# A fused graph-attention and transformer kernel: four steps moved at the seam between attention and feed-forward

## What is computed

```python
gamma1, gamma2, scale1, scale2, shift1, shift2 = ada(silu(cond))
x1 = _ln(x) * (scale1 + 1.0) + shift1
q, k, v = x1 @ mat_qkv_w.T + qkv_bias              # 16 heads of 16
q = _l2norm(q) * exp(min(scale_mul, log 100)); k = _l2norm(k)
o = softmax(q @ k.T) @ v
x = x + (o @ proj_w.T + proj_b) * gamma1           # "projection", "gate", "residual"
x2 = _ln(x) * (scale2 + 1.0) + shift2
h = gelu(x2 @ fc1_w.T + fc1_b)                     # 256 -> 1024
x = x + (h @ fc2_w.T + fc2_b) * gamma2             # 1024 -> 256
```

## Time and profile before

| | us |
|---|---|
| time of three runs | 797.12, 798.02, 800.97 (median 798.02) |
| the profiled execution | 799.24 |
| its span in the trace | 797.5 |
| PE busy | 732.4 (92% of the span) |
| DVE / ACT / POOL busy | 500.0 / 444.0 / 323.0 |

### The profile page before, as it was taken

One profiled execution on the slowest core, in us unless ns is written; L12 is line 12 of the kernel. 1 busy time (PEld: TensorE's weight loads), 2 busy tenths in 40 slices (PEclk: granted clock), 3 DMA queues, 4 the chain that ended last, 5 costly groups with the idle time before them and its releaser, 6 DMA issues.

```text
span 797.5 us, 15010 instructions
## 1 busy us (share of the span) xinstructions
PE 732.4 (92%) x4708; PEld 521.8 (65%) x4708; DVE 500.0 (63%) x1047; ACT 444.0 (56%) x733; POOL 323.0 (41%) x550
## 2 busy tenths in 40 slices
PE   4799999999996689999999999998598999999997
PEld 2587778888873345555555555555357888888885
DVE  2158999989987757767676767665414444444432
ACT  0335555555543367766666666666455555555553
POOL 1024655655653245555555555544542202222100
PEclk9989999999999899999999999999779999999999
DMA  8831333333311777667666666677400000000001
GB/s 236 293 93 39 111 100 107 114 97 109 101 32 53 128 156 147 148 147 154 141 153 147 150 147 144 147 145 146 76 14 1 14 27 14 27 28 27 14 27 39
DMA packets 83096, 79.65 MB, mean 100 GB/s; under 512 B 22942, under 2 KB 71710, under 8 KB 83054
## 3 DMA queue, kind: packets, MB, share of 16 engines
q1 hardware_dynamic: 81726, 78.95, 41.2%
q10 hardware_dynamic: 1328, 0.16, 0.1%
HBM read 57.13 MB, written 21.66 MB: 99 GB/s over the span
## 4 chain that ended last, share of the span: by engine, by line
PE 53%; ACT 5%; DVE 3%; DMA 3%; issue 2%; POOL 2%; SPq 1%; ACTq 0%; DVEq 0%; POOLq 0%
PE ps L1667 11%; PE ps L1681 11%; PE ps L1488 7%; PE ps L1560 5%; PE ps L1546 5%; PE ps L1598 3%; ACT probsT L903 3%; PE ps L1498 3%; PE ps L1579 2%; PE ps L1514 1%; DMA k_stack<-parts_dram 1%; PE ps L1652 1%; PE ps L1591 1%; ACT part_pairs L926 1%; DMA gate_rows<-rows_dram 1%
## 5 line engine op out<-in xcount | busy, mean ns | idle before, releaser
L903 ACT ACTIVATE probsT<-ps 128x1024 f32<-128x1024 f32 x128 | 130.5, 1019 | 31.5 <-PE ps L1546 31.5
L1303 DVE TENSOR_TENSOR hidden_low<-hidden,hidden_high 128x512 fp32r<-128x512 f32 x64 | 46.1, 720 | 110.1 <-ACT hidden_high L997 61.6
L994 ACT ACTIVATE hidden<-ps,b_fc 128x512 f32<-128x512 f32 x64 | 44.1, 689 | 74.1 <-PE ps L1667 74.1
L1546 PEld LDWEIGHTS ps<-q_stack,k_stack 49*128 49x128 f32 x512 | 39.4, 190 | 61.6 <-ACT probsT L903 37.1
L1560 PE MATMUL ps<-probsT,v_ones 128*32 128x256 f32 x1024 | 70.5, 395 | 4.7 <-ACT probsT L903 4.5
L1546 PE MATMUL ps<-q_stack,k_stack 49*128 49x256 f32 x512 | 66.1, 337 | 8.7 <-ACT probsT L903 7.6
L691 POOL TENSOR_TENSOR scores<-scores,row_max 128x640 f32<-128x640 f32 x32 | 42.1, 1317 | 77.1 <-DVE row_max L1033 77.1
L1196 DVE TENSOR_REDUCE neg_max<-ps 128x4 bf16<-128x344 f32 x128 | 59.4, 506 | 15.2 <-PE ps L1514 15.2
L1488 PE MATMUL ps<-w_qkv,x1T 128*128 128x512 f32 x128 | 64.7, 628 | 3.2 <-DVE part_pairs L1203 3.2
L1406 PE MATMUL ps<-x_res,w_q 128*128 (+1 forms) x256 | 65.2, 401 | 0.0
L1406 PEld LDWEIGHTS ps<-x_res,w_q 128*128 128x128 f32 x256 | 48.5, 199 | 11.5 <-issue 5.4
(11 more groups left out here) (181 smaller groups left out, 1709.3 us busy)
## 6 DMA issues: line engine op xcount, KB each, us to landing
parts_dram<-part_pairs SPq DMA_DIRECT2D x64, 256.0 KB
q_stack<-parts_dram SPq DMA_DIRECT2D x96, 128.0 KB, 5.4
k_stack<-parts_dram SPq DMA_DIRECT2D x96, 128.0 KB, 5.8
adj<-in_adj SPq DMA_DIRECT2D x16, 440.0 KB, 3.5
xT<-in_xT SPq DMA_DIRECT2D x16, 256.0 KB, 2.8
x_res<-in_x SPq DMA_DIRECT2D x16, 256.0 KB, 3.4
x_in<-in_x SPq DMA_DIRECT2D x16, 256.0 KB, 2.7
gate_rows<-rows_dram SPq DMA_DIRECT2D x16, 256.0 KB, 7.1
```

Source lines behind the costliest of these rows:

```text
L903: nc.scalar.activation(probsT[:, s % 4, :], ps[:, COLS:COLS + 2, :].rearrange("p a n -> p (a n)"), ACT.Exp).then_inc(exp_made, 1)
L994: nc.scalar.activation(hidden[:, s % RAW, :], ps[:, FC1[s % FC1_BANKS], :], ACT.Gelu, bias=b_fc1[:, m:m + 1]).then_inc(gelu_made, 1)
L1303: nc.vector.tensor_tensor(hidden_parts[1][:, s % H_SLOTS, :], hidden[:, s % RAW, :], hidden_parts[0][:, s % H_SLOTS, :], ALU.subtract).the ...
L1546: mm = nc.tensor.matmul(ps[:, COLS + j, kt * N:(kt + 1) * N], k_stack[at, par, s, kt * P:(kt + 1) * P], q_stack[at, par, s, :], start=True ...
```

## The change

No work is added or removed. In turn 16 POOL runs the split of the first feed-forward weight ahead of `bias(13)` and not behind it; `ffn_root(0)` stays behind both, now with `bias(13)` right ahead of it. In turn 17 alone, batch 14's way back starts in slot 1 (`back_at`): each of its steps but the residual is two slots sooner; `first_x2(1)` moves from slot 0 to slot 2, behind `divide`. And for pair 1 alone the statistics, moments, normalisation, transposes and scaling move from steps 0 to 3 to steps 2 to 5 (`norm_at`).

```diff
-    NORM_AT = 3
+    def norm_at(n):
+        return 3 if n else 5
...
+    def back_at(c):
+        return 1 if isinstance(c, int) and c == B - 1 else 3
...
         def turn(f, b, c, d, par):
             ahead = following(f)
+            if isinstance(c, int) and c == B - 2:
+                pool.wait_ge(g["late_weights"], g["LATE"])
+                split(w_fc1, w1_high, w1_low, w1_split)
             if ahead is not None:
                 norm_root(pool, nc, ahead, mean_var, g, var_eps, rstd, mv_made, eps_made, rstd_made)
...
             if isinstance(c, int) and c == B - 2:
-                pool.wait_ge(g["late_weights"], g["LATE"])
-                split(w_fc1, w1_high, w1_low, w1_split)
                 ffn_root(0)
...
-                if d is not None and s == 4:
+                if d is not None and s == back_at(c) + 1:
                     add_bias_v(d)
...
-                if d is not None and s == 3:
+                if d is not None and s == back_at(c):
                     divide(d)
-                if d is not None and s == 6:
+                if d is not None and s == back_at(c) + 3:
                     gate(d)
...
                     first_x2(0)
+                if isinstance(c, int) and c == B - 1 and s == 2:
                     first_x2(1)
...
-                if m == 0:
+                if m == norm_at(n) - 3:
                     statistics(n + 1)
-                if m == 1:
+                if m == norm_at(n) - 2:
                     ffn_moments(n + 1)
-                if m == 2:
+                if m == norm_at(n) - 1:
                     ffn_normalise(n + 1)
...
-                if d is not None and s == 3:
+                if d is not None and s == back_at(c):
                     output_tokens(d, f)
...
-                if d is not None and s == 4:
+                if d is not None and s == back_at(c) + 1:
                     output_channels(d, f)
-                if d is not None and s == 5:
+                if d is not None and s == back_at(c) + 2:
                     project(d)
...
-            if m == NORM_AT and n + 1 < PAIRS:
+            if m == norm_at(n) and n + 1 < PAIRS:
                 ffn_norm(n + 1)
```

## The result

Median of seven runs each: 798.08 us before (796.10 to 800.97), 794.00 us after (790.12 to 797.62); the ratio is 0.9948 with a 95% interval of 0.9924 to 0.9973. Two later timings of the same two kernels gave 798.13 and 791.92 (0.9928, 0.9909 to 0.9948) and 797.61 and 792.81 (0.9938, 0.9913 to 0.9963). So the change makes the kernel faster, by 4 to 6 us and not by 11, and 794.0 lies above the range of 784.5 to 792.0.

A forecast was written before the change was run, and what follows sets the result against it. PE, busy 92% of the span, was taken to bound the kernel through its work, gaps and lowered clock. Gains 5.0 + 1.0 + 2.9 + 1.9 = 10.8 us took 798.02 to 787.2, rounded 787.0; range 784.5 to 792.

The forecast's parts named there:

- Part 1: Turn 16: the split ahead of the bias on POOL removes PE's wait for `x_hat_f`; gain 5.0 us.
- the new neighbours of the split: Turn 16: DVE work beside POOL's split, taken as 0; slower rival, split holds DVE, 801 us, chance 0.04.
- the row of gates: Turn 16: the root still hangs on it; rival, landing 5 us later loses half of Part 1, 790 us, chance 0.03.
- Part 2: Start of turn 17: the pair's transposes run at full clock instead of half; gain 1.0 us.
- Part 3: Turn 17: batch 14's way back two slots sooner, at full clock, 19.5 us instead of 22.44; gain 2.9 us.
- turn 17 gives nothing: Rival: ACT's exponentials with its other work set turn 17's length and gaps only move; 790 us, chance 0.08.
- Part 4: First feed-forward steps: pair 1's normalisation two steps later shortens PE's waits at `o_tok` and the transposes; gain 1.9 us.
- The clock: Rival: the clock falls again in turn 17, half clock for about 8 us, costing 5 us; 792 us, chance 0.13.
- The forecast's own range: 784.5 to 790 us, from the bounds of Part 3 (0 to 5.5), of Part 4 and of the landing (0 to 1.7).
- the landing: Start of turn 17: batch 15's stacks arriving late for PE's column scores; bounds 0 to 1.7 us, taken as 0.

The follow-up runs named there:

- part 1 not made: Three traced executions of the kernel before (799.24, 798.70, 798.31 us) and one with only pair 1's normalisation moved two steps later (796.17 us).
- kernels with fillers: Changed kernel plus extra static-data matmuls in PE's gaps of turns 16 and 17: 789.57, later 790.00 us; without Part 3, 790.23, later 789.98 us.

## Why the prediction was wrong

**The forecast that the change makes the kernel faster was right, its size wrong**: 11 us forecast, 4 to 6 measured.

**Part 1 (5.0 us): right for the profiled execution, wrong as a term for the median.** The mechanism came as laid out: the split fills POOL's wait, the root ends at 562.4 (forecast 562.5), `x_hat_f` is ready before PE, and neither the new neighbours of the split nor the row of gates cost anything; the maxima took what they had taken (482 to 518 ns). The failed step is that a wait read in one execution was taken off the median of all. Two of the four traced executions with part 1 not made had 5.0 us of it, two had 0.18 and 0.58. Alone it measured 2.1 us (0.8 to 4.1).

**Part 2 (1.0 us): right in size against a half clock**, 0.9 in the profiled execution; worth nothing against those executions of before that came there at full clock (1.02 us from transposes to column scores in its third).

**Part 3 (2.9 us): wrong.** The layout of the new order was right (19.5 laid out, 19.52 and 19.51 measured). The failed step was the subtraction: 22.44 us at half clock, less 19.5 at full clock, put down to the order. The old order should have been laid out at full clock in the same way; it takes 19.38. The rival "turn 17 gives nothing" had this right, in that the gaps only moved; its reason, that ACT sets the turn's length, is not shown (ACT was busy 11.65 us of either order's turn at full clock).

**Part 4 (1.9 us): right**, 2.2 in every trace with it; the wait at `o_tok` became 0.39 (forecast 0.43), the one at pair 1's transposes went, and pair 1's first step came 6.5 us after the transposes (forecast 6.4).

**The clock: the rival that came true, with a chance of 0.13.** It was priced at 5 us and cost 2.5 in the profiled execution (22.06 against 19.5). The argument against it, that 550 to 560 had kept 1.00 with PE at 7.84 of 10, was one execution's luck: in seven of the eleven rows of the table above the clock did fall in turn 16. That it would fall there was in no term and in no rival.

**What is missing, added up.** From the key blocks to the end the profiled execution of before took 247.2 us; less the forecast's 10.8 that is 236.4. The kernels with fillers and a full clock came to 236.1, 236.2 and 236.8. So the sum as a whole was right for that execution with the clock at full, and for a wrong reason in part 3: its 2.9 us were the clock's. The changed kernel's five traces took 238.7 to 242.9, 240.6 in the mean, which is 4.2 us above the forecast; and the four with part 1 not made were 245.6 in the mean (with 2.2 us added for part 4), 1.6 below the one from which the forecast started. The two make 5.8 us of the 10.8 and leave 5.0, as the medians say. These are means of few traces. That the profiled execution of after, 790.30 us, came near the 788.4 forecast for it does not speak for part 3, whose term failed by 2.5 us in it. As for the filled kernels' medians of 790 where 787 was forecast, in their four traces turn 16 began at 549.3 to 554.5 us, and the one that began at 549.3 had the wait for the stacks.

The forecast's own range also had a slip: with part 3 worth nothing and the landing at 1.7 us late its bounds give 791.8 and not 790.

The Trainium skill, page "TensorE: Matmul & The Clock Gate", section "Part 1: The HAM clock gate", says that activity releases the throttle and, of a kernel's start, that the number of matmuls at the low clock varies from run to run of one kernel. The table shows such variation in mid-kernel: one kernel, falls in turn 16, in turn 17 or in both. The same skill's page "SBUF — State Buffer", section "Who interferes with whom", says that a VectorE operation with two inputs in SBUF contends with a GpSimd operation that reads SBUF. The residual of batch 13, which has two such inputs, took 1.31 us beside the split and 0.69 without it, and agrees.

## What to carry to other kernels

A wait ahead of a stage absorbs what is late on the waiting engine before it, so removing it is worth the wait of each execution and not the wait of the one that was profiled: read two or three executions before taking it off the median. Compare executions from a mark just before the change, so that what varies ahead of it drops out. Never subtract a layout at full clock from a stretch that was measured at half clock; lay out both orders at the same clock, and see whether the order is worth anything. Where PE waits in slot after slot for another engine, as here, count on the clock falling in some executions. Short extra matmuls that fit in the gaps, timed first, held it in three of the four traces of the changed kernel with them.

## What had not been expected of the hardware

The clock falls at places that differ from execution to execution of one kernel. The kernel before showed two mixtures: none in turn 16 and 16.8 us at half clock behind it, or 6.9 and 7.0 us. The second is 3.2 us shorter from the start of turn 16 on (244.0 against 247.2), which their times (798.3 and 798.7) hide, since that turn began 2.8 us later in it. An f32 matmul of 256 columns, issued once, stands as two in the trace and takes 0.48 us at full clock (four in 1.92 us), or 0.44 in the row of ten. DVE's normalisation took 2.26 us beside `bias(14)` on POOL and 1.37 or 1.38 without it.
